# A graph layer on one core: TensorE gathers five batches of edges per 30 groups instead of ten

## The reference

```
msg  = relu(x[src] + edge_attr @ We + be)            # 200000 x 128
aggr = segment_sum(msg, dst, num_segments=6250)
h    = (1 + eps) * x + aggr
h    = relu(h @ W1 + b1) @ W2 + b2
h    = (h - mean(h)) * rsqrt(var(h) + 1e-5) * gamma + beta    # over the nodes
out  = layernorm(x + relu(h) + x)                    # over the 128 values
```

## Time and profile before

| | us |
|---|---|
| timed runs, median (lowest, highest) | 1582.13 (1579.88, 1583.58) |
| profiled execution, span | 2684.1 |
| TensorE matmuls busy | 1871.5 |
| TensorE weight loads busy | 1369.8 |
| GpSimd busy | 1154.5 |
| VectorE busy | 991.5 |
| ScalarE busy | 841.5 |

### The profile page before, as it was taken

The page is one execution under the profiler, slowest core; times in us unless marked ns, Lnnn a source line. Parts: engine busy times, 40 slices in busy tenths (PEclk is TensorE's granted clock), DMA queues, the critical chain, the costliest instruction groups (busy, mean ns, idle before and its releaser), DMA issues.

```text
span 2684.1 us, 58837 instructions
## 1 busy us (share of the span) xinstructions
PE 1871.5 (70%) x23395; PEld 1369.8 (51%) x23395; DVE 991.5 (37%) x3361; ACT 841.5 (31%) x1954; POOL 1154.5 (43%) x1193
## 2 busy tenths in 40 slices
PE   1776777776777777677767767767767776766776
PEld 0455555555555555555555555555555555555554
DVE  6433333333333333333333333333333333333335
ACT  3232323232332333232323323323223322322335
POOL 6444444444444444444444444434434444444421
PEclk9877788787887787788888778878778778887888
DMA  8222222232222222222222222222222222222221
GB/s 231 62 59 65 62 59 68 59 71 66 63 63 61 61 62 64 61 66 59 67 61 61 65 61 63 65 58 65 64 58 67 61 62 63 63 65 62 62 86 50
DMA packets 148455, 180.61 MB, mean 67 GB/s; under 512 B 41677, under 2 KB 128932, under 8 KB 147924
## 3 DMA queue, kind: packets, MB, share of 16 engines
q1 hardware_dynamic: 102489, 89.62, 14.0%
q0 software_dynamic: 37728, 77.31, 11.5%
q10 hardware_dynamic: 7963, 9.90, 1.2%
HBM read 170.09 MB, written 6.63 MB: 66 GB/s over the span
## 4 chain that ended last, share of the span: by engine, by line
PE 66%; issue 20%; another core or an unknown queue 8%; ACT 2%; DVE 1%; ACTq 0%; DVEq 0%
PE ps L1330 23%; PE ps L1315 15%; PE ps L1255 12%; PE ps L1269 11%; PE ps L1296 1%; PE ps L1276 1%; PE ps L1299 1%; ACT xg L694 1%; PE ps L1287 1%; PE ps L1384 1%; ACT slotS L680 0%; PE ps L1288 0%; PE ps L1394 0%; DVE lnst L1197 0%
## 5 line engine op out<-in xcount | busy, mean ns | idle before, releaser
L574 POOL DMA_INDIRECT xg<-xb,idxb x1145 | 1106.6, 966 | 1423.9 <-DVE msg L937 1068.8
L1330 PE MATMUL ps<-iota_all 128*128 128x128 bf16 x4032 | 377.8, 247 | 425.7 <-issue 291.3
L688 ACT ACTIVATE iota_all<-ps 128x384 bf16<-128x384 f32 x896 | 408.5, 489 | 775.6 <-remote 567.8
L1330 PEld LDWEIGHTS ps<-iota_all 128*128 128x128 bf16 x4032 | 290.1, 111 | 515.6 <-issue 511.5
L1022 DVE TENSOR_TENSOR accT<-accT,ps 128x64 f32 x390 | 86.5, 222 | 1138.4 <-remote 992.8
L1255 PE MATMUL ps<-we,ea 64*128 64x128 f32 x3126 | 344.2, 367 | 45.7 <-issue 45.3
L1330 PE MATMUL ps<-iota_all,hot_all 128*128 128x128 bf16 x4032 | 301.1, 229 | 102.6 <-issue 98.8
L937 DVE TENSOR_TENSOR msg<-ps,xg 128x512 f32<-128x512 f32 x390 | 262.0, 686 | 238.9 <-PE ps L1255 233.2
L1330 PEld LDWEIGHTS ps<-iota_all,hot_all 128*128 128x128 bf16 x4032 | 247.2, 102 | 172.4 <-issue 145.0
L1255 PEld LDWEIGHTS ps<-we,ea 64*128 64x128 f32 x3126 | 288.0, 261 | 80.7 <-issue 72.2
L1269 PE MATMUL ps<-msg,hot 128*64 128x128 f32 x3120 | 300.9, 352 | 6.2 <-issue 4.5
(11 more groups left out here) (135 smaller groups left out, 1113.8 us busy)
## 6 DMA issues: line engine op xcount, KB each, us to landing
ea<-in_eat SPq DMA_DIRECT2D x156, 320.0 KB
lowB<-lowD SPq DMA_DIRECT2D x128, 224.0 KB
xg<-xb,idxb POOLq DMA_INDIRECT x1145
accT<-in_xt ACTq DMA_DIRECT2D x1, 3125.0 KB
x<-in_xt ACTq DMA_DIRECT2D x1, 3125.0 KB
iota_all<-in_x ACTq DMA_DIRECT2D x1, 3080.0 KB
out<-iota_all SPq DMA_DIRECT2D x5, 512.0 KB
xb<-iota_all SPq DMA_DIRECT2D x3, 784.0 KB, 6.2
```

The costliest lines, as they stand in the source:

```text
L574: pool.indirect_dma_start(out=xg[0:rows, slot, j, :], out_offset=None, in_=of, in_offset=bass.IndirectOffsetOnAxis(ap=index, axis=0)).then ...
L688: act.activation(rows3[:, t, :, :].rearrange("p a h -> p (a h)"), ps_rows(k * NTILE + t), ACT.Copy)\
L1330: last = pe.matmul(found[:, e, :], sel2[set_of(k)][:, t, e * P:(e + 1) * P], rows3[:, t, a, :], start=(t == 0 and e == 0 and a == 0), stop ...
```

## The change

SORTED has five groups of the 30 instead of ten, every sixth instead of every third: 2, 8, 14, 20, 26. In the other five GpSimd gathers all four tiles, so that it gathers 105 of the 120 tiles of an iteration, where it gathered 90. The start visits (FIRST) move with the groups, a cycle of source columns is six groups long, with the batch's three tiles at its third group (PICKED), and K1 = 3 leaves one batch out at the end of the last iteration, that of group 26. All else follows from these numbers.

```diff
-    SORTED = (2, 5, 8, 11, 14, 17, 20, 23, 26, 29)
+    SORTED = (2, 8, 14, 20, 26)
...
-    FIRST = tuple(3 * k - 3 for k in range(NB))
+    FIRST = tuple(6 * k - 3 for k in range(NB))
...
-    CYCLE = 3 * GROUP
-    K1 = 7
+    CYCLE = 6 * GROUP
+    PICKED = 3 * GROUP - HALF
+    K1 = 3
...
-        assert all(g % 3 == 2 for g in SORTED) and ROUND % 3 == 0
+        assert all(g % 6 == 2 for g in SORTED) and ROUND % 6 == 0
...
-                    .rearrange("p (m c) -> p m c", c=CYCLE)[:, :, CYCLE - HALF:CYCLE]
+                    .rearrange("p (m c) -> p m c", c=CYCLE)[:, :, PICKED:PICKED + HALF]
```

## The result

| | us |
|---|---|
| before, timed, median of 4 (range) | 1582.34 (1579.88 to 1583.58) |
| after, timed, median of 4 (range) | 1795.61 (1792.27 to 1798.05) |
| after / before | 1.1342, 95% interval 1.132 to 1.1364 |
| forecast | 1820 (1775 to 1835) |

The kernel became 213 us slower. The direction, the engine that binds and the range of the forecast held; the likeliest value lay 24 us too high. So it is the width of the whole range that took it in.

A forecast was written before the change was run, and what follows sets the result against it. GpSimd was taken to bound the kernel before and after: 54.8 + 1337*1.271 + 5 + 39 = 1798 us, with the 24 us around it 1822, equally 1582.1 + 240; put at 1820, range 1775 to 1835.

The forecast's parts named there:

- Which engine binds: Whole kernel: GpSimd binds before (floor 1558 us against TensorE's 1421) and after; chance 0.72.
- Price of an added gather: GpSimd's gathers of `xb`: 0.966 + 0.305 = 1.271 us each, 189 more on the path, +240.2 us.
- the rival on the side of faster: Gap between gathers: its 0.30 us exists only while the profiler records, a gather takes 0.966, time 1414 us; chance 0.08.
- Three gathers hidden at the start: First ten groups: three added gathers of `in_x` end by about 51 us, hidden by the store of `xb`.
- Batches removed, worth nothing: Batches 128 to 64: TensorE loses 422 us (400 to 450), none of it on the path.
- Point 3 of the prediction: VectorE's selects, run half as often, could disturb fewer gathers: at most 0.022 us each, 29 us; none taken.
- The 24 us left over: GpSimd's sum of 1558 against the median before: launch, program end and brief ring waits, kept after the change.
- The first rival: TensorE binds before, GpSimd afterwards: GpSimd's 24 idle us vanish, 1798 us (range 1769 to 1808); chance 0.17.
- theory T: Kernel before: the 24 us missing from GpSimd's sum are its waits for the loaded TensorE.
- Clock: TensorE's clock may fall after the change; at half clock it needs 25.1 of 26.7 us per three steps, not binding.
- The neighbours in `ring_of`: Steps 30 and 31 share bank 3: about 1 us in 13 places, 13 us on TensorE, hidden by its slack.
- The span that should fall: Recorded span, 2684.1 us before: should fall, since the recording is TensorE-bound and TensorE has half the batches.

The follow-up runs named there:

- e: The kernel before, unchanged, recorded once more: 1577.81 us in the one timed run, span 1575.9.
- c: The kernel before with two gathered tiles of four in groups without a batch from the second iteration on, 480 gathers fewer: 1479.31 us, 0.9348.
- b: The kernel before with only 28 of 56 picks and 7 of 63 joins of a batch on TensorE: 1577.85 us, 0.9966.
- d: The kernel before, ten batches kept, with the change's 192 added gathers going into a buffer that nobody reads: 1815.12 us, 1.1471.
- a_half_batches: The kernel before with the changed kernel's five batches on TensorE, but gathers kept near the kernel before (1185 against 1179): 1575.62 us, 0.9954.
- f_few_selects: d with VectorE's selects cut from the third batch on, to one of two (line 989) and one of seven (line 1000): 1793.62 us, 1.1346.
- h: The changed kernel with four more select instructions a batch on VectorE, whose results nobody reads: 1804.5 us, 1.1421.
- k: The kernel before, full computation, with the one-hot compare (line 920) replaced by eight compares of one SBUF input and a scalar: 1567.18 us, 0.9912.

## Why the prediction came out as it did

The two undisturbed recordings give the whole difference, in us:

| | before (e) | after | difference |
|---|---|---|---|
| first gather of `xb` begins | 55.0 | 56.5 | +1.5 |
| gathers of `xb` | 1148 | 1337 | 189 * 1.269 = +239.8 |
| mean gather with its gap | 1.282 | 1.269 | 1148 * 0.0131 = -15.0 |
| waits for a slot | 3.1 | 0 | -3.1 |
| end of the last gather to the end | 46.8 | 43.8 | -3.0 |
| span | 1575.9 | 1796.0 | +220.1 |

The timed medians are 213.3 us apart. The recorded executions took 1577.81 and 1798.05, 4.5 below and 2.4 above their medians, and that is the rest.

**Which engine binds: right, shown.** GpSimd's floor against TensorE's was the step that carried the sign. c, b and e show it: TensorE's own pace was 1479 (worked out: 1446), relieving it brings 5 us, and a slot is waited for 3.1 us.

**Price of an added gather: right.** 1.271 worked out from a recording in which GpSimd was busy 43% of the time; 1.269 after. The gap of 0.30 us is real in timed runs too, so the rival on the side of faster fell; it needed a gather below 1.091 us. That the price fits so well is in part luck: the kernel before, undisturbed, has 1.282, and the disturbed recording happened to lose nearly as much a gather as the changed kernel does (the table below).

**Three gathers hidden at the start: nearly.** They were to end by 51 us, before `xb` was ready. They came under the long adds of the start (line 1016, 2.0 us each) and lasted 2.0 to 2.4 us; GpSimd reached `xb` at 56.48 and lost the 1.5 us.

**Batches removed, worth nothing: wrong in size.** This is the term that was mis-sized. Point 3 of the prediction saw that selects could lengthen a gather, gave 29 us as the most, and took none, because the only case it had looked at was the compare of line 920, "whose count stays". Measured: 19.5 us between d and the changed kernel, or 15.0 in the gathers' length between the undisturbed recordings of before and after. Where they go is seen from the gathers after 90 us, by what VectorE runs 0.2 us after their start (number of gathers, and the us that they last beyond 944 ns, added up):

| | under the compare | under the selects |
|---|---|---|
| before, first recording | 63, 18.0 | 54, 2.7 |
| before (e) | 74, 14.9 | 238, 14.5 |
| a_half_batches | 72, 17.0 | 119, 10.7 |
| d_more_gathers | 85, 19.7 | 262, 19.3 |
| f_few_selects | 76, 17.2 | 50, 2.5 |
| after | 43, 10.0 | 116, 9.6 |

The recording that the price was read from met a select 54 times, an undisturbed one 238 times: so the selects looked harmless, and 977 ns were read as 966. Against d the changed kernel gains about 10 us under the selects, whose number it halves, and about 10 under the compare, which it runs as often. The count of the compare stayed, what it cost did not. That selects lengthen gathers is shown by f and h; why the compare meets half as many gathers in the changed kernel is not shown.

**The 24 us left over: wrong.** I carried them over to the other kernel as launch, end and brief waits. Between span and timed run there are 1.9 us (1577.81 against 1575.9, 1798.05 against 1796.0). 12.6 are 1148 gathers at 1.282 instead of 1.271, about 3 the end, 3 the slot; the last few are the median over the recorded run. Only the 1.9 had to stay after the change: the sum without the 24 was 1798, 2 us from the measured span. This is the same error as the one before, seen in the total: half of the 24 were the longer gathers. The first rival had the right number, 1798, for a wrong reason, theory T.

**Clock.** TensorE's granted clock fell as foreseen, from 0.98 in the stretch 75 to 1500 us of e to 0.81 in 75 to 1700 us of the changed kernel, with TensorE busy 95% and then 67% of it, and did not bind (us; busy of PE, PEld, DVE, ACT, POOL; clock, DMA):

```profile
75.00:1500.00 1425.00, 1356.05 (x22992) 1054.10 (x22989) 918.12 (x3096) 749.13 (x1847) 1083.05 (x1113) 0.98 0.47 112
...
75.00:1700.00 1625.00, 1087.41 (x14510) 854.81 (x14508) 680.87 (x2016) 513.39 (x1196) 1233.66 (x1285) 0.81 0.41 93
```

**The neighbours in `ring_of`: right.** TensorE's pick matmuls wait for ScalarE's copies 7.1 us in all in the changed kernel, and the path does not run through them.

**The span that should fall: right for a wrong reason.** I took the recording as what slowed TensorE. It did not: d, with as many matmuls and more instructions, was recorded in 1814.5 us and e in 1575.9. The first recording was one disturbed execution. What held TensorE back in it stays open; it did not come again in eleven recordings, the changed kernel's among them. With an undisturbed page the Trainium skill's ranking (Perfetto Trace Analysis, Identifying the Most-Contended Engine) puts GpSimd with 74% before TensorE's weight loads with 70%, the other way round than the earlier trace rows: here the rule names the engine that binds, once the page it is applied to is not a disturbed one.

Open: why a_half_batches, with the changed kernel's work on VectorE and 186 gathers fewer, loses more in its gathers (28.7 us against 21.8 from 75 us on). The table has nearly all of it under the compare, 72 gathers against 43. So it is how the gathers fall in time against VectorE; what sets that was not tried. Nor was a compare that reads one input from PSUM, which by the rows of line 937 would hold no gather up.

## What to carry to other kernels

Before a change moves work onto an engine, add up that engine's instructions with the gaps between them: GpSimd was full at 74% busy, because 0.30 us behind each indirect DMA of 0.94 count as idle. Where a recorded execution is much longer than a timed one, take durations from it and record it again before trusting waits, shares or the frequency with which engines meet. A part of a sum that is left over belongs to a place; carried to the new kernel unexplained, it was as large as the whole error here. And a count with a limit (gathers over 1.0 us) can hide the rule: to hold the end of the one instruction against the end of the other showed it.

## What the runs showed of the hardware that I had not expected

An indirect DMA on GpSimd that begins while VectorE runs certain instructions is held until that instruction ends, and ends 0.81 to 0.83 us after it; alone it lasts 0.944. So it loses up to 0.5 us under the compare of 0.68 us, and 1.4 here, under an add of 2.0 us with two inputs in SBUF at the start of the changed kernel:

```profile
50.65 2.03 DVE L1016 TENSOR_TENSOR iota_all<-iota_all,x 112x1792 f32<-112x1792 f32 x1 [0.63 <-DMA xb<-iota_all]
51.14 2.35 POOL L575 DMA_INDIRECT xg<-in_x,idxb  x1 [0.30 <-issue]
```

Three forms do this: two float32 inputs in SBUF (53 of 53 in e), the selects from float16 to bfloat16 (101 of 118 in e), and a float32 input in SBUF with a scalar (16 of 18 in k). The add with one input in PSUM does not (34 in e, 77 after, none over 0.95 us). By the count at 0.2 us that add has 1 slow gather of 278 in the changed kernel but 27 of 206 in e; each of these has a select in the same gather.

The Trainium skill (SBUF — State Buffer, SBUF: two separate sides) states that GpSimd and VectorE share a port pair, which the one that begins first has for its whole instruction: on VectorE's side an instruction in a 2-port mode or, against a GpSimd instruction that reads SBUF, one with two SBUF inputs. The measured ends agree with it, and so does the add under which nothing is held. In which mode the selects and the one-input compares ran no run shows.

The way out is short instructions: to spend 148 us more of VectorE's time, in eight compares where there was one, made the kernel 13.5 us faster.
